# Feed-forward products of a tile moved by some pairs of steps in a fused attention kernel

## Time and profile before

| | us |
|---|---|
| median of 3 runs (1714.85 to 1716.05) | 1715.87 |
| the profiled execution | 1716.38 |
| its span, first to last instruction | 1714.6 |
| PE busy | 1705.3 (99%) |
| DVE busy | 1491.8 (87%) |
| ACT busy | 1327.6 (77%) |
| POOL busy | 707.7 (41%) |

### The profile page before, as it was taken

One profiled execution on the slowest core, in us unless ns is written; L12 is line 12 of the kernel. 1 busy time (PEld: TensorE's weight loads), 2 busy tenths in 40 slices (PEclk: granted clock), 3 DMA queues, 4 the chain that ended last, 5 costly groups with the idle time before them and its releaser, 6 DMA issues.

```text
span 1714.6 us, 44336 instructions
## 1 busy us (share of the span) xinstructions
PE 1705.3 (99%) x17862; PEld 1145.5 (67%) x17862; DVE 1491.8 (87%) x2276; ACT 1327.6 (77%) x1683; POOL 707.7 (41%) x947
## 2 busy tenths in 40 slices
PE   9999999999999999999999999999999999999999
PEld 5666666666666666666666666666666666666666
DVE  5788988898889888888898888888888889898884
ACT  3438888888888888888888888888888888888872
POOL 1003334554433345544333555443335554333455
PEclk9999999999999999999999999999999999999999
DMA  6851112111211221112111211221122112211133
GB/s 201 273 186 40 38 54 55 46 37 54 55 51 32 54 55 44 39 54 55 47 36 54 55 41 42 54 55 45 37 55 55 38 45 55 55 41 41 42 104 102
DMA packets 95390, 108.02 MB, mean 63 GB/s; under 512 B 56016, under 2 KB 70224, under 8 KB 95184
## 3 DMA queue, kind: packets, MB, share of 16 engines
q1 hardware_dynamic: 91728, 101.97, 20.7%
q10 hardware_dynamic: 3456, 3.21, 0.6%
HBM read 78.91 MB, written 20.97 MB: 58 GB/s over the span
## 4 chain that ended last, share of the span: by engine, by line
PE 98%; DVE 1%; DMA 0%; issue 0%; ACTq 0%; ACT 0%; SPq 0%
PE banks L672 30%; PE ring L648 21%; PE ring L655 15%; PE ring L661 14%; PE banks L771 6%; PE banks L776 5%; PE banks L599 3%; PE ring L861 2%; PE ring L611 1%; PE ring L590 1%; PE ring L563 0%; DVE pmax L931 0%; DMA attnT<-x 0%; PE banks L823 0%; DVE stats L880 0%; PE ring L577 0%
## 5 line engine op out<-in xcount | busy, mean ns | idle before, releaser
L509 ACT ACTIVATE probs<-ring 128x1024 f32<-128x1024 f32 x1024 | 1002.9, 1026 | 13.3 <-PE ring L661 6.5
L648 PE MATMUL ring<-kst,qst 64*128 64x512 f32 x2000 | 673.7, 417 | 0.0
L947 DVE TENSOR_REDUCE pmax<-ring 128x2 f32<-128x1024 f32 x500 | 611.2, 1222 | 38.3 <-PE ring L648 21.6
L672 PE MATMUL banks<-probs,vst 128*32 128x256 f32 x8192 | 548.2, 385 | 0.1
L515 ACT ACTIVATE half_sb<-ring 128x512 f32<-128x512 f32 x500 | 299.5, 599 | 265.8 <-PE ring L648 258.4
L655 PE MATMUL ring<-qst,kst 64*128 64x512 f32 x2048 | 490.6, 429 | 1.0 <-DVE pmax L947 0.5
L648 PEld LDWEIGHTS ring<-kst,qst 64*128 64x128 f32 x2000 | 329.7, 184 | 211.4 <-issue 205.3
L661 PE MATMUL ring<-shift_rows,ones 64*128 64x512 f32 x2048 | 421.7, 390 | 0.0
L936 DVE TENSOR_REDUCE pmax<-ring 128x1 f32<-128x512 f32 x500 | 345.1, 690 | 83.3 <-PE ring L648 80.2
L942 DVE TENSOR_REDUCE pmax<-half_sb 128x1 f32<-128x512 f32 x500 | 334.9, 670 | 35.9 <-ACT half_sb L515 30.4
L672 PEld LDWEIGHTS banks<-probs,vst 128*32 128x32 f32 x8192 | 213.7, 109 | 211.3 <-issue 90.4
(11 more groups left out here) (86 smaller groups left out, 939.3 us busy)
## 6 DMA issues: line engine op xcount, KB each, us to landing
kst<-qk_scratch SPq DMA_DIRECT2D x256, 128.0 KB, 3.0
qst<-qk_scratch SPq DMA_DIRECT2D x256, 128.0 KB, 2.9
qk_scratch<-attnT SPq DMA_DIRECT2D x32, 256.0 KB, 3.1
shift_rows<-shiftT SPq DMA_DIRECT2D x512, 2.0 KB
qk_scratch<-probs SPq DMA_DIRECT2D x16, 256.0 KB, 3.0
attnT<-o_turned SPq DMA_DIRECT2D x256, 16.0 KB, 1.9
xnT<-x SPq DMA_DIRECT2D x8, 512.0 KB, 5.4
out<-xnT SPq DMA_DIRECT2D x7, 512.0 KB, 3.2
```

Of the source, the lines that this page charges most:

```text
L509: act.activation(probs[:, s % PS, :], score_slot(g), ACT.Exp, scale=SCALE).then_inc(exp_done, 1)
L648: return pe.matmul(unit_slot(g)[:, c * BLK:(c + 1) * BLK], qst[b][rows, tile * P:(tile + 1) * P], kst[b][rows, key:key + BLK], start=True, ...
L672: mm = pe.matmul(po[32 * j:32 * (j + 1), half * D:(half + 1) * D], vst[b][:, kt, :], quarters[:, j], start=(kt == 0), stop=(kt == TB - 1))
L947: dve.tensor_reduce(pmax[:, tile, 2 * part:2 * part + 2], unit_slot(g).rearrange("p (c e) -> p c e", c=2), AX, ALU.max).then_inc(mx_taken, 1)
```

## The change

It moves the whole feed-forward schedule so that a tile's products lie within its own unit: first products at s = 0 to 14, second products at s = 16 to 30 of unit i. Against the old order that is six steps, three pairs, later. ACT's copies go to steps 7, 15 and 31. POOL's first square moves from the end of one unit (behind LIF) to the next one (behind LIF and the copy of v). `first_up` goes: the first three pairs have shares like all others. The last unit has shares to the end. `use` counts from 0, and the two waits of SP name the same fillings by their new numbers. The core of the diff:

```
         def use(i, k):
-            return USES * i + 2 + k
-
-        DOWN, UP_A, UP_B = range(USES)
+            return USES * i + k
+
+        UP_A, UP_B, DOWN = range(USES)
...
                 if last:
-                    sp.wait_ge(misc_full, use(i - 1, UP_B) + 1)
+                    sp.wait_ge(misc_full, use(i, UP_B) + 1)
...
-            square(0, 0, UP_A)
             def head(h, b, last=False):
                 i = 2 * h + b
                 if not last:
                     stage_v(h + b, 1 - b, STEPS * i + PS)
+                square(i, 0, UP_A)
                 square(i, 1, UP_B)
...
-                if not last:
-                    square(i + 1, 0, UP_A)
...
-                    if s == 9:
+                    if s == 7:
+                        take_up(i, 0, UP_A)
+                    if s == 15:
                         take_up(i, 1, UP_B)
-                    if s == 25:
+                    if s == 31:
                         act.wait_ge(misc_full, use(i, DOWN) + 1)
                         act.wait_ge(lif_done, i + 1)
                         act.activation(y_sb[:], misc[:, 0:D], ACT.Copy).then_inc(misc_taken, 1)
-                    if s == 33 and not last:
-                        take_up(i + 1, 0, UP_A)
...
-            def head(h, b, last=False):
-                i = 2 * h + b
-                def share(s, side, c):
+            def share_of(i, s, last):
+                def share(side, c):
                     opens, ends = (side, c) == (1, 0), (side, c) == (0, 1)
                     if opens and last and s > LEAD:
                         pe.wait_ge(score_ready, STEPS * i + s)
-                    elif opens:
+                    elif opens and (i or s):
                         pe.wait_ge(mx_ready, FIRST_MAX + STEPS * i + s)
                     if (side, c) == (0, 0):
-                        pe.wait_ge(upper_share, TB * i + (s - FIRST) // 2 + 1)
-                    if s in (6, 8):
-                        mm = up(i, 6 + (s - 6) // 2, side, c)
-                        if ends and s == 8:
+                        pe.wait_ge(upper_share, TB * i + s // 2 + 1)
+                    if s == 0 and i and opens:
+                        pe.wait_ge(misc_taken, use(i, UP_A))
+                    if s == 8 and opens:
+                        pe.wait_ge(misc_taken, use(i, UP_B))
+                    if s <= 14:
+                        mm = up(i, s // 2, side, c)
+                        if ends and s in (6, 14):
                             mm.then_inc(misc_full, 1)
-                    if s == 10 and opens:
+                    if s == 16 and opens:
                         pe.wait_ge(misc_taken, use(i, DOWN))
                         pe.wait_ge(squared, 2 * i + 3)
...
-                    if s == 18 and opens:
+                    if s == 24 and opens:
                         pe.wait_ge(squared, 2 * i + 4)
-                    if 10 <= s <= 24 and c == 0:
-                        mm = down((s - 10) // 2, side)
-                        if side == 0 and s == 24:
+                    if s >= 16 and c == 0:
+                        mm = down((s - 16) // 2, side)
+                        if side == 0 and s == 30:
                             mm.then_inc(misc_full, 1)
...
-                    if s >= 26:
-                        mm = up(i + 1, (s - 26) // 2, side, c)
-                        if ends and s == 32:
-                            mm.then_inc(misc_full, 1)
...
-                    pair(h, b, s, last, (lambda side, c: share(s, side, c)) if s <= 24 or not last else None)
+                    pair(h, b, s, last, share_of(i + s // STEPS, s % STEPS, last) if s < STEPS or not last else None)
...
+            pe.wait_ge(lo_done, QB * NB + QK_BANKS)
             for s in range(0, FIRST, 2):
-                pair(0, 0, s, between=lambda: first_up(s))
+                pair(0, 0, s, False, share_of(0, s, False))
```

More of the change, by code:

```diff
@@ L349, in _ @@
             head(H - 1, 0)
-            sp.wait_ge(misc_full, use(3 * NT // 4 - 2, UP_B) + 1)
+            sp.wait_ge(misc_full, use(3 * NT // 4 - 1, UP_B) + 1)
             for t in END_EARLY:
@@ L406, in square @@
                 c = slice(part * FC // 2, (part + 1) * FC // 2)
-                pool.wait_ge(misc_taken, use(tile - 1, k) + 1)
+                pool.wait_ge(misc_taken, use(tile, k) + 1)
                 pool.tensor_tensor(hid_sb[:, c], relu_sb[:, c], relu_sb[:, c], ALU.mult).then_inc(squared, 1)
-            square(0, 0, UP_A)
             def head(h, b, last=False):
@@ L517, in take_up @@
             def take_up(tile, part, k):
-                act.wait_ge(misc_full, use(tile - 1, k) + 1)
+                act.wait_ge(misc_full, use(tile, k) + 1)
                 act.wait_ge(squared, 2 * tile + part + 1)
@@ L547, in _ @@
                         act.wait_ge(stored[w][0], 32 * (NB // 2))
-                    take_up(0, 0, UP_A)
                 exponentials(s, s)
@@ L694, in score_free, with pair @@
                     pe.wait_ge(exp_done, x + 2)
-            def pair(h, b, s, last=False, share=None, between=None):
+            def pair(h, b, s, last=False, share=None):
                 i = 2 * h + b
@@ L750, in pair @@
                     shifted(g + 1, odd, 1, 1)
-                if between:
-                    between()
                 if ahead:
@@ L806, in share @@
                             mm.then_inc(misc_full, 1)
[L807 to L810, removed]
-                    if s >= 26:
-                        mm = up(i + 1, (s - 26) // 2, side, c)
-                        if ends and s == 32:
-                            mm.then_inc(misc_full, 1)
-                    if side == 1 and c == (0 if 10 <= s <= 24 else 1):
+                    if side == 1 and c == (0 if s >= 16 else 1):
@@ L816, in share, with head @@
                         mm.then_inc(upper_share, 1)
+                return share
+            def head(h, b, last=False):
+                i = 2 * h + b
                 for s in range(FIRST, STEPS + FIRST, 2):
-                    pair(h, b, s, last, (lambda side, c: share(s, side, c)) if s <= 24 or not last else None)
[L821 to L825, removed]
+                    pair(h, b, s, last, share_of(i + s // STEPS, s % STEPS, last) if s < STEPS or not last else None)
```

## The result

Median 1723.03 us (1722.56 to 1723.35, 6 runs) against 1715.36 (1714.70 to 1716.93, 6 runs of the kernel before beside them): ratio 1.0042, 95% interval 1.0031 to 1.0053, so 7.7 us slower. The forecast was 1715.4 in a range to 1718.6.

A forecast was written before the change was run, and what follows sets the result against it. TensorE was taken as the bound (98% of the chain of waits). Start −2.35, units 0, last unit +1.43 and +0.27, end +0.2 summed to −0.45 us, carried to median 1715.87: 1715.4, range 1713.6 to 1718.6.

The forecast's parts named there:

- The start: First three pairs: one block per pair in place of two gains 2.6 us, less a 0.25 longer pair: net −2.35.
- Units 0 to 30, nothing: Units 0 to 30: the same long pairs and y copy at other steps, cost 0, kept to ±1.0 us.
- the bumps: Pairs behind ACT's 0.60 us feed-forward copies, 0.25 us longer than others, twice a unit; said to move to other steps.
- POOL. Cost 0: POOL's LIF, copy of v and first square before the second products: 22.6 of 25.1 us needed, 2.5 left, cost 0.
- Rival 2: POOL late for the second products: the 2.5 us margin gone, one us beyond costs 30 (1746); chance 0.03.
- The last unit's shares and the y copy: Last unit: added shares cost 1.43 us (0.9 to 1.9), y copy before the last exponential 0.27 (0 to 0.39).
- The end: Final projection: VectorE waits for the last LIF, TensorE does not, two stores leave late; 0.2 us (0 to 1.5).
- Rival 1: Pair 8: VectorE's cast also waits for POOL, shift links late; full 21 us (1736), chance 0.10; mild 1717, chance 0.12.
- rival 3: End: last tile's LIF ends past +24.5, sums fall behind the projection, up to 2 us (1717.4); chance 0.07.
- rival 4: Pair 8: VectorE's links and ACT's copy overlap, a long pair partly hides, 31 × 0.25 gained (1707.6); chance 0.05.

The follow-up runs named there:

- Experiment 6: Kernel before the change, whole blocks of the first three pairs moved behind the odd step's maxima; one run, 1712.55 us, those pairs 11.46 in place of 12.22.
- experiment 1: Changed kernel with TensorE's wait for the shift rows of pairs 0 and 16 moved ahead of the pair's first maximum; 1717.99 us, ratio 1.0011 to the kernel before.
- experiment 8: Kernel of experiment 3 with one more POOL tensor_scalar at the start of every LIF, moving the rest 0.92 us later; 1713.60 us, ratio 0.9993.
- experiment 3: Changed kernel with the shift-row wait moved earlier and the last unit's six early bias additions moved from step 10 to 18; 1713.84 us, ratio 0.9990.
- experiment 5: Kernel before the change with a satisfied TensorE wait added ahead of the first scores in pairs 4 and 12, which no copy lengthens; 1715.44 us, ratio 0.9999.
- experiment 4: Kernel before the change with a satisfied TensorE wait added ahead of the first scores in pairs 2 and 10, which ACT's copies lengthen; 1719.47 us, ratio 1.0023.

## Why the prediction was wrong

- **The start** (forecast −2.35 net) was right: −2.88 + 0.33 = −2.55. Its working took about 0.8 from the order, VectorE's late odd reduction, and the rest from the blocks themselves (1.1 in the second pair, and a third pair of 3.04 in place of 4.06). Experiment 6 gives 0.76 and 2.1. Pair 4 starts 6.30 behind the first pair; the forecast was 6.3 to 6.7.
- **"Units 0 to 30, nothing": the step that failed in the middle is its list of what the bumps newly meet.** The bumps did move whole, as forecast, and the waits on the feed-forward bank did keep their distances. What the list lacks is TensorE's own wait for the shift rows. The kernel's text shows it in just the pairs 0 and 16, and with the copies at steps 31 and 15 both late exponentials fall there. It cost 5.1 us in all, 0.17 a unit, by experiment 1; against the trace before, these units are 4.2 longer (the forecast said 0 ± 1.0).
- **"POOL. Cost 0": right in the middle, failed in the last unit.** In the middle (unit 15, kernel after) the first square ends at 874.87 and its use begins at 877.49: 2.6 of margin, forecast 2.5.

```profile
873.83 1.04 POOL L408 TENSOR_TENSOR hid_sb<-relu_sb 128x512 f32<-128x512 f32 x1
```
```profile
877.49 0.18 PEld L770 LDWEIGHTS banks<-wproj_sb,hid_sb 64*128 64x128 f32 x1
```

I gave the one number of the middle units to all 31. In the last one the shorter pairs leave 1.4 of it, and LIF of tile 30 is stretched by 3.9. The prediction had seen the last tile's LIF stretch by 2.7 beside VectorE's large operations, and did not look for the same at step 10, where six bias additions stand. Rival 2 named the mechanism with 0.03 and "in the middle its end never moves". Its price per microsecond was by the 30 units, while it struck in one: 2.6 of stand, and 1.6 behind it at the lower clock, which no rival had.
- **The last unit's shares and the y copy** (+1.43 and +0.27): right. Unit 31 takes 44.96 with the stand away, 1.69 over the 43.27 of before; the three shares alone are 1.33. The y copy's part was not measured by itself.
- **The end** (0.2): right. VectorE waits 2.95 for the last LIF (forecast some 4) and the stretch is as long as before, to 0.05:

```profile
1710.71 0.40 POOL L436 CAST counts<-lif 128x256 bf16<-128x256 f32 x1
```
```profile
1711.21 1.23 DVE L1022 SCALAR_TENSOR_TENSOR xnT<-counts,xnT 128x1024 f32<-128x1024 bf16 x1 [2.95 <-POOL counts L436]
```

- **Rival 1** (the cast waits) did not come in units 1 to 30, but not for the reason that I gave. The operation is not too short: it waited as soon as POOL's instruction was a tensor_tensor. That it met a tensor_scalar in all of these units is luck of LIF's phase. The prediction's reading that an operation with two SBUF inputs waits for POOL's current instruction came from a tensor_tensor and was too wide: after the change the scaling takes 0.28 beside a tensor_scalar in 31 units. The Trainium skill ("SBUF — State Buffer", section "Who interferes with whom") says that a cast can take the port pair that VectorE shares with GpSimd. The traces agree beside POOL's tensor_tensor (0.33 to 0.41 in experiment 8) and not beside its tensor_scalar (0.17).
- **Rivals 3 and 4** did not come: LIF of the last tile ends 21.7 behind the start of the projection, under the 24.5 of rival 3, and pair 8 has the whole bump (3.288), where rival 4 had part of it hidden.

All in all there were 5.1 + 4.1 = 9.2 us of losses that the forecast did not have. The rest of the change gains 1.6 (experiment 3), and 9.2 − 1.6 is 7.6, where 7.7 was measured.

## What to carry to other kernels

When a step moves, list every wait of the bounding engine that stands where the step's disturbance will land: a wait that has always been satisfied is free only as long as the wait beside it is satisfied too. Check a margin in each regime that has other work beside it, the last unit above all, not in the typical one alone. And where a short job on a second engine lengthens a whole period, cut the job until it fits the period's slack.

## What the runs showed of the hardware that was not expected

- A satisfied wait of TensorE costs nothing beside a satisfied one (experiment 5), and 0.09 us a time ahead of one that comes late (3.29 to 3.38, experiment 4). The profile puts such a wait down to "issue".
- VectorE's scaling with two SBUF inputs took 0.50 to 0.60 beside POOL's tensor_tensor (31 times before the change), and 0.28 beside POOL's tensor_scalar (31 times after it). There is one exception, in the last unit before the change: 0.48 beside a tensor_scalar that was itself stretched. In the other direction the tensor_scalar did suffer: 1.71 in place of 0.85 there, and beside the bias additions after the change (1660.27). Why the kind matters was not tried.

```profile
1686.77 0.48 DVE L1027 TENSOR_TENSOR o_scaled<-o_sb,rden 128x128 f32<-128x128 f32 x1
```
```profile
1685.85 1.71 POOL L430 TENSOR_SCALAR lif<-lif 128x256 f32<-128x256 f32 x1
```

- Behind the one stand of 2.4 us TensorE worked at its lower clock for a while (granted 0.76 over the 7 us, matmuls of 0.62 in place of 0.39); in the kernel without the stand the clock stayed at 1.00 there.
